# Attention values as float32 matmuls in four column groups, and the first layer norms' normalisation moved from VectorE to GpSimd

## What is computed

```python
xn = layer_norm(layernorm(x), norm_g, norm_b)          # (32, 128, 128)
xfn = layer_norm(ctx_768, tnorm_g, tnorm_b)            # (32, 77, 96)
q, k, v = xn @ Wq + bq, xfn @ Wk + bk, xfn @ Wv + bv   # 16 heads of 8
w = softmax(q @ k.T / sqrt(8))
x = x + tanh(g_xattn) * (w @ v)
xf = layernorm(x)
top_vals, top_idx = top_k(xf @ w_router, 2)            # of 8 experts
h = square(relu(xf @ w1[e]))                           # for every expert
y = sum over the two chosen of (h @ w2[e]) * softmax(top_vals)
x = x + tanh(g_ffn) * y
```

## Time and profile before

| what | before |
|---|---|
| median of 3 runs | 432.58 us (431.52 to 435.71) |
| profiled execution | 432.84 us |
| its span on the core | 431.0 us |
| mean granted TensorE clock | 0.761 |
| busy: TensorE, VectorE, ACT, GpSimd | 72%, 68%, 52%, 51% |

### The profile page before, as it was taken

One profiled execution on the slowest core, in us unless ns is written; L12 is line 12 of the kernel. 1 busy time (PEld: TensorE's weight loads), 2 busy tenths in 40 slices (PEclk: granted clock), 3 DMA queues, 4 the chain that ended last, 5 costly groups with the idle time before them and its releaser, 6 DMA issues.

```text
span 431.0 us, 9014 instructions
## 1 busy us (share of the span) xinstructions
PE 309.2 (72%) x2664; PEld 261.7 (61%) x2664; DVE 291.7 (68%) x956; ACT 224.9 (52%) x490; POOL 221.8 (51%) x261
## 2 busy tenths in 40 slices
PE   0502693779399849885997869885888599699566
PEld 0301472667388738874786748774777488587455
DVE  5524744875577787868785787877887678847432
ACT  1210353556356765676565646764576467665222
POOL 8601353664566555755573458545754565665100
PEclk9965555555559975998598958995999589769869
DMA  2346019001831075206530382229211821050140
GB/s 51 100 87 93 2 44 142 5 2 42 143 125 75 33 116 157 106 28 105 159 119 8 78 170 75 75 75 159 96 75 57 146 97 78 27 198 2 47 174 24
DMA packets 29314, 36.57 MB, mean 85 GB/s; under 512 B 5849, under 2 KB 22874, under 8 KB 29274
## 3 DMA queue, kind: packets, MB, share of 16 engines
q1 hardware_dynamic: 28474, 35.05, 33.1%
q0 software_dynamic: 512, 1.06, 0.9%
q10 hardware_dynamic: 288, 0.00, 0.0%
HBM read 23.14 MB, written 2.23 MB: 59 GB/s over the span
## 4 chain that ended last, share of the span: by engine, by line
PE 39%; DVE 23%; issue 13%; DMA 11%; SPq 5%; POOL 4%; ACT 3%; DVEq 1%; POOLq 0%; ACTq 0%
PE y L533 10%; DMA qs<-q_lo 8%; PE ab L455 6%; PE s L477 5%; SPq L313 4%; DVE u L947 3%; DVE negm L831 3%; PE c L493 3%; DVE xn L782 3%; PE h L524 2%; PE ab L437 2%; DMA gb<-gates_scratch 2%; PE h L526 2%; PE h L525 2%; DVE x L867 2%
## 5 line engine op out<-in xcount | busy, mean ns | idle before, releaser
L1079 POOL TENSOR_TENSOR p_lo<-p,p_hi 77x512 f16<-77x512 f32 x128 | 147.8, 1158 | 109.9 <-ACT p L681 109.7
L831 DVE TENSOR_REDUCE negm<-ab 128x4 f32<-128x308 f32 x128 | 58.9, 470 | 72.7 <-PE ab L455 69.8
L455 PE MATMUL ab<-ks,qs 96*128 96x312 f32 x128 | 62.8, 495 | 39.8 <-DMA qs<-q_lo 27.4
L680 ACT ACTIVATE p_hi<-s 77x512 f16<-77x512 f32 x128 | 74.8, 585 | 31.2 <-PE s L477 30.9
L533 PE MATMUL y<-w2s,hs 128*128 128x128 f32 x512 | 74.2, 293 | 6.1 <-ACT hs L688 6.0
L477 PEld LDWEIGHTS s<-qs,ks 104*77 104x77 f32 x512 | 70.1, 194 | 10.9 <-issue 4.8
L681 ACT ACTIVATE p<-s 77x512 f32<-77x512 f32 x128 | 74.8, 584 | 0.0
L533 PEld LDWEIGHTS y<-w2s,hs 128*128 128x128 f32 x512 | 67.5, 206 | 8.1 <-ACT hs L688 7.4
L477 PE MATMUL s<-qs,ks 104*77 104x128 f32 x512 | 72.0, 280 | 0.2 <-ACT p L681 0.2
L455 PEld LDWEIGHTS ab<-ks,qs 96*128 96x128 f32 x128 | 31.1, 244 | 47.0 <-issue 33.9
L688 ACT ACTIVATE hs<-u 128x512 f32<-128x512 f32 x64 | 40.2, 628 | 31.3 <-DVE u L947 29.1
(11 more groups left out here) (100 smaller groups left out, 503.7 us busy)
## 6 DMA issues: line engine op xcount, KB each, us to landing
gb<-gates_scratch SPq DMA_DIRECT2D x16, 768.0 KB, 4.2
qs<-q_hi SPq DMA_DIRECT2D x16, 256.0 KB, 5.7
gb<-gates_scratch SPq DMA_DIRECT2D x8, 512.0 KB, 3.6
ks<-k_hi SPq DMA_DIRECT2D x64, 39.0 KB
x_sb<-in_x_dram SPq DMA_DIRECT2D x8, 256.0 KB, 6.7
qs<-q_lo SPq DMA_DIRECT2D x8, 256.0 KB, 6.9
x_res<-in_x_dram SPq DMA_DIRECT2D x8, 256.0 KB, 6.8
out_dram<-y_out SPq DMA_DIRECT2D x8, 256.0 KB, 5.8
```

Of the source, the lines that this page charges most:

```text
L455: nc.tensor.matmul(p[:, 0:J * NP].rearrange("t (i n) -> t i n", n=NP), qs[0:QR, par, c, T * j:T * j + T], ks[0:QR, par, c, :, NP * j:NP * ...
L680: nc.scalar.activation(p_hi[:, c, :], src, ACT.Exp).then_inc(hi_done, 1)
L831: nc.vector.tensor_reduce(negm[:, :, c], bank_ab[bank][:, 0:J * NP].rearrange("t (i n) -> t i n", n=NP)[:, :, 0:N], AX.X, ALU.max, negate= ...
L1079: nc.gpsimd.tensor_tensor(p_lo[:, c, :], p32[:, c, :], p_hi[:, c, :], ALU.subtract).then_inc(lo_done, 1)
```

## The change

1. **Exponentials.** ACT writes only `p32`; `p_hi`, `p_lo` and GpSimd's `low_part` are gone.
2. **Values.** The roles are turned round: `vs` is stationary and `p32` moves, both plain float32. Each head has 32 stationary columns, of which either the first 16 or the last 16 are used (8 features, the ones, 7 zeros) and the others are zero. The four heads of a chunk go to partitions 0, 32, 64 and 96 of bank `c`, which are four column groups of the array. Two chunks add into the same 128 columns, one with the first 16 rows of every group, the other with the last 16. The output has features on partitions.
3. **Turning back.** ACT copies the 128x256 of bank `c` to `oT` (`evacuate_heads`), TensorE turns it in two transposes (`turn_heads`) into a bank `ab`, with four new uses in `AB_USES`, and VectorE's reciprocal and multiplication read from there. The addition of the three parts is gone.
4. **v.** ACT writes v straight into `vs` in two instructions (even and odd heads); the three splitting steps are gone. GpSimd clears `vs` and writes the ones at the start.
5. **First layer norms.** GpSimd runs `normalise` (four instructions for the context, four for x) right behind each root; VectorE's `normalise_ctx` and `normalise_x` are gone. VectorE's `take(post)` is one place later.

```diff
-        vs = sb("vs", [N, 2, G, H, VC], BF16)
+        vs = sb("vs", [N, 2, G, H, VT])
-        p_hi = sb("p_hi", [N, LR, CH * T], F16)
-        p_lo = sb("p_lo", [N, LR, CH * T], F16)
+        oT = sb("oT", [CH * VT, 2 * T])
...
@@ -483,17 +475,27 @@
                 if c == 0:
-                    pe.wait_ge(split_v, at(SPLIT, s, "lo"))
+                    bank, k = ab(s, "v")
+                    pe.wait_ge(v_done, s + 1)
+                    pe.wait_ge(ab_taken[bank], k)
+                    if not loop and n == 0:
+                        pe.wait_ge(v_ones, ONES)
                     if loop or n > 0:
-                        pe.wait_ge(post_d, at(POST, n - 1, "recip"))
-                pe.wait_ge(lo_done, m + 1)
+                        pe.wait_ge(o_taken, n)
+                pe.wait_ge(p_done, m + 1)
+                r = T * (c // 2)
                 for i in range(J):
-                    h, k = NC * i + c, T * i
-                    for part in (p_hi, p_lo):
-                        mm = nc.tensor.matmul(bank_c[:, VC * h:VC * h + VC], part[:, c, k:k + T],
-                                              vs[:, par, j, h, :], start=(c == 0 and i == 0 and part is p_hi),
-                                              stop=(part is p_lo), skip_group_check=True)
+                    mm = nc.tensor.matmul(bank_c[VT * i:VT * i + VT, r:r + T], vs[:, par, j, NC * i + c, :],
+                                          p32[:, c, T * i:T * i + T], start=(c == 0), stop=(c % 2 == 1),
+                                          skip_group_check=True)
                 mm.then_inc(pv_done, 1)
+
+            def turn_heads(s, par, j, loop=False):
+                pe.wait_ge(o_taken, G * s + j + 1)
+                p, ready = claim(s, f"o{j}", loop)
+                for r in range(2):
+                    mm = nc.tensor.transpose(p[:, T * r:T * r + T], oT[:, T * r:T * r + T], ident[:, :])
+                mm.then_inc(ready, 1)
...
@@ -556,6 +558,8 @@
                         scores(*near[2], 3, loop)
                     if near[0]:
                         scoresT(*near[0], 1, loop)
+                    if near[-1]:
+                        turn_heads(*near[-1], loop)
                     if e[0] is not None:
                         hidden(sf, pf, e[0], loop)
...
-                nc.scalar.activation(vs[:, par, :, :, 0:HD * PARTS].rearrange("n b h (d a) -> n a (b h) d", a=PARTS)[:, 0],
-                                     bank_ab[bank][0:N, :].rearrange("n (c d) -> n c d", d=HD), ACT.Copy,
-                                     scale=col(GX, N)).then_inc(hi_v, 1)
-                if loop or s > 0:
-                    act.wait_ge(split_v, at(SPLIT, s - 1, "rest"))
-                nc.scalar.activation(v32[:, :, :].rearrange("n b d -> n (b d)"), bank_ab[bank][0:N, :], ACT.Copy,
-                                     scale=col(GX, N)).then_inc(ab_taken[bank], 1)
+                for odd, done in enumerate((v_done, ab_taken[bank])):
+                    k = VC * odd
+                    nc.scalar.activation(vs[:, par].rearrange("n b (m o) k -> n o (b m) k", o=2)[:, odd, :, k:k + HD],
+                                         bank_ab[bank][0:N, :].rearrange("n (m o d) -> n o m d", o=2, d=HD)[:, odd],
+                                         ACT.Copy, scale=col(GX, N)).then_inc(done, 1)
+
+            def evacuate_heads(s, par, j):
+                act.wait_ge(pv_done, NC * (G * s + j) + NC)
+                nc.scalar.activation(oT[:, :], bank_c[:, 0:2 * T], ACT.Copy).then_inc(o_taken, 1)
...
@@ -677,7 +685,6 @@
                 if loop or m >= LR:
                     act.wait_ge(pv_done, m - LR + 1)
                 src = bank_s2[c % 2][0:N, :]
-                nc.scalar.activation(p_hi[:, c, :], src, ACT.Exp).then_inc(hi_done, 1)
                 nc.scalar.activation(p32[:, c, :], src, ACT.Exp).then_inc(p_done, 1)
...
                 dve.wait_ge(stats_d, at(STATS, s, "x_stats"))
+                if loop or s > 0:
+                    dve.wait_ge(normed, at(NORM, s - 1, "x_normed"))
...
@@ -845,26 +817,25 @@
             def attended(s, par, j, loop=False):
 
                 n = G * s + j
-                dve.wait_ge(pv_done, NC * n + NC)
-                view = bank_c[:, 0:VC * H].rearrange("t (h v) -> t h v", v=VC)
-                nc.vector.tensor_reduce(o[:, :].rearrange("t (h d) -> t h d", d=HD),
-                                        view[:, :, 0:HD * PARTS].rearrange("t h (d a) -> t h d a", a=PARTS),
-                                        AX.X, ALU.add).then_inc(post_d, 1)
+                bank, k = ab(s, f"o{j}")
+                view = bank_ab[bank][:, 0:VC * H].rearrange("t (h v) -> t h v", v=VC)
+                dve.wait_ge(ab_ready[bank], k)
                 nc.vector.reciprocal(rden[:, :].rearrange("t (h o) -> t h o", o=1),
-                                     view[:, :, HD * PARTS:VC]).then_inc(post_d, 1)
+                                     view[:, :, HD:HD + 1]).then_inc(post_d, 1)
                 yield
                 dve.wait_ge(post_d, at(POST, n, "recip"))
-                nc.vector.tensor_tensor(o[:, :].rearrange("t (h d) -> t h d", d=HD),
-                                        o[:, :].rearrange("t (h d) -> t h d", d=HD),
+                nc.vector.tensor_tensor(o[:, :].rearrange("t (h d) -> t h d", d=HD), view[:, :, 0:HD],
                                         rden[:, :].rearrange("t (h o) -> t h o", o=1).broadcast_to([T, H, HD]),
-                                        ALU.mult).then_inc(post_d, 1)
+                                        ALU.mult).then_inc(ab_taken[bank], 1)
                 yield
                 if j == 0:
                     dve.wait_ge(res_in[par], landed(s, par))
                     if loop or s >= 2:
                         dve.wait_ge(y_added, s - 1)
-                dve.wait_ge(post_d, at(POST, n, "scaled"))
-                nc.vector.tensor_tensor(x1[:, par, j, :], x_res[:, par, j, :], o[:, :], ALU.add).then_inc(post_d, 1)
+                dve.wait_ge(ab_taken[bank], k)
+                nc.vector.tensor_tensor(x1[:, par, j, :].rearrange("t (i r e) -> t i r e", i=J, r=2),
+                                        x_res[:, par, j, :].rearrange("t (i r e) -> t i r e", i=J, r=2),
+                                        o[:, :].rearrange("t (r i e) -> t i r e", i=J, r=2), ALU.add).then_inc(post_d, 1)
...
-                    if j == 1 and nxt:
-                        prepare = split_values(*nxt, loop)
-                    if j == 3 and third:
-                        prepare = chained(normalise_ctx(*third, loop), normalise_x(*third, loop))
...
-                    take(post)
                     take(top_scores)
                     if near[-2]:
                         routed(*near[-2])
                     take(top_scores)
+                    take(post)
                     take(post)
                     if near[-2]:
...
-            def low_part(s, par, j, c):
-
-                m = NC * (G * s + j) + c
-                pool.wait_ge(hi_done, m + 1)
-                pool.wait_ge(p_done, m + 1)
-                nc.gpsimd.tensor_tensor(p_lo[:, c, :], p32[:, c, :], p_hi[:, c, :],
-                                        ALU.subtract).then_inc(lo_done, 1)
+            def normalise(s, par, which):
+                src, dst, n, mv, k, name = {"ctx": (ctx_sb, cn, N, c_mv, 1, "crstd"),
+                                            "x": (x_sb, xn, T, x_mv, 3, "rstd")}[which]
+                pool.wait_ge(norm_p, at(NORM_P, s, name))
+                apart(pool)
+                for b in range(G):
+                    ins = nc.gpsimd.tensor_scalar(dst[:, b, :], src[:, par, b, :], mv[:, b, 0:1],
+                                                  nrm[0:n, k, b:b + 1], ALU.subtract, ALU.mult)
+                ins.then_inc(normed, 1)
...
+            nc.gpsimd.memset(vs[:, :, :, :, :], 0.0).then_inc(v_ones, 1)
+            pool.wait_ge(v_ones, 1)
+            for odd in range(2):
+                k = VC * odd + HD
+                nc.gpsimd.memset(vs[:, :, :, :, :].rearrange("n p b (m o) k -> n o (p b m) k", o=2)[:, odd, :, k:k + 1],
+                                 1.0).then_inc(v_ones, 1)
...
@@ -1123,20 +1097,13 @@
                         load_experts()
                     if j == 3 and third:
                         norm_rstd(third[0], "ctx")
-                    if near[0]:
-                        low_part(*near[0], 0)
-                    if j == 3 and third:
+                        normalise(*third, "ctx")
                         norm_rstd(third[0], "x")
+                        normalise(*third, "x")
                     if j == 1 and exists(i - 1, loop):
                         gate_roots(i - 1)
-                    if near[0]:
-                        low_part(*near[0], 1)
                     if near[-1]:
                         rstd(*near[-1])
-                    if near[0]:
-                        low_part(*near[0], 2)
-                    if near[0]:
```

(1 more changed line is left out.)

80 lines of the change are left out of this document (21 added, 59 removed).

## The result

The changed kernel takes 468.21 us (median of four runs, 464.73 to 470.78), the kernel before beside it on the same chip 432.05 us (431.19 to 435.71). The ratio is 1.081, with a 95% interval of 1.072 to 1.091: 36 us slower. The prediction said 436 us, range 419 to 472. The time lies inside the range, and the sign that I held likelier came; the case that I called likeliest did not. The trace of the changed kernel is of the fastest of its four runs, 464.73 us: its span is 462.9 us where the kernel before has 431.0, so the traces show 31.9 of the 36 us.

A forecast was written before the change was run, and what follows sets the result against it. Bound by transfers (some 19 us of each 45 us tile) and TensorE's work (some 26). TensorE stretches +5.1, two earlier ones +2, beginning +2 and -2, end -4.5 and +1: +3.6 on 432.84, 436 us (chance 0.35); range 419 to 472.

The forecast's parts named there:

- the sign that I held likelier: Whole kernel slower than before by over 1%: chance 0.50, against 0.30 faster and 0.20 within 1%.
- What bounds the kernel: Per 45 us tile, some 19 us set by transfers up to q_lo (transfer stretch), some 26 by TensorE's work (TensorE stretch).
- Chunks at 0.22 us, groups beside each other: Values of four heads on TensorE: column groups overlap, 0.22 us at full, 0.43 at half clock; +0.9 us per TensorE stretch.
- the drain rival: Each values chunk pays two TensorE drains of 0.15 us for changing tiling mode; 16 us more, 452; chance 3%.
- Turning, 0.24 us per batch, "I count no wait": Two TensorE transposes per batch turn heads back: 0.24 us full, 0.48 half clock, no wait for ACT's copy; 0.96 per stretch.
- The clock stays as it is: First 10 of a TensorE stretch's 25.7 us stay at half clock; about four chunks run at half, seven at full.
- Half of the 8.5 us idle comes back: TensorE stretches: half of the 8.5 us idle over five stretches comes back as shorter waits, -4.2 us.
- GpSimd's normalisations, 0.45 us each: 64 layer-norm normalisations moved to GpSimd: 0.45 us each, 6.2 us with the roots, in a slot of 11 us.
- Beginning and end: Beginning: about +2 us for clearing and normalisations, -2 for lost p_lo latency; end: -4.5, +1 for chunks and turns.
- Rival 1: Slower: passes in program order, only neighbouring column groups overlap; chunk 0.54 us full, 1.05 half clock; 467 or 460; chance 0.20.
- Rival 2: Slower: column groups do not overlap; chunk 0.86 us full, 1.68 half clock; 497 or some 480 us; chance 0.15.
- Rival 3: Faster: all stretch idle, end's 4.7 us and beginning's 4 us go, chunks stay 0.20 us; -12.4, 420 us; chance 0.27.

The follow-up runs named there:

- e10: Changed kernel without the heads' copy and turning transposes (attention values wrong), normalisations back on VectorE; 443.8 us, 1.018 of the kernel before.
- e3: Changed kernel with the heads turned later, behind the third scoresT, and VectorE's part behind the gating; 464.6 us, 1.072 of the kernel before.
- e12: Changed kernel with normalisations back on VectorE and the heads turned behind the slot's first hidden layer; 458.4 us, 1.056 of the kernel before.
- e4: Changed kernel with all four heads of a chunk in one column group (three quarters of attention values left out); 548.6 us, 1.264 of the kernel before.

## Why the prediction was right and wrong, step by step

- **What bounds the kernel** (two stretches per tile): right. The transfer stretch kept its 17.7 us, q_lo's wait took the gates' place, and every steady us lost is in the TensorE stretch.
- **Chunks at 0.22 us, groups beside each other**: right for a chunk in the middle of a visit. At half clock two chunks take 1.02 us (271.38 to 272.40), twice the forecast's 0.43 and 0.16 for the exit. The step lacked the price of entering and leaving, 0.22 us per visit. I had weighed it as the drain rival, read the earlier trace rows as showing none, and gave it 3%. A cost of that kind exists, at about three quarters of the 0.30 us that I put on it, but paid per visit, not per chunk; whether it is a drain stays open. By itself it decided little: e10, which has all visits, has before's period, since the waits that went pay for them.
- **Turning, 0.24 us per batch, "I count no wait"**: this step failed, and it is the largest part of the miss against 436 us. I looked for ACT's copy of bank c, and rightly found it hidden (383 ns, 0.2 us of waits in all). I didn't ask for the other half of the claim, the bank itself. The use before the last is the router's, which VectorE takes behind 0.48 us of maxima. The runs show 0.88 us per turn instead of 0.24. With VectorE's normalisations, leaving the turning out is worth 21 of 29 us. The wait is shown by the trace; that it is most of the 21 us is not, as moving it away brought back only 4 to 5 us (e3, e12), and part of the rest is the clock.
- **The clock stays as it is** ("the idle time before it stays"): the premise held, 4.49 us of idle time for 3.38 and 0.88, and the conclusion did not in two of the four tiles. The half-clock part after the first scores lasted 15.2 and 14.1 us, not 10, and 8.0 and 9.7 in the other two; in e10 it lasted about 9. Six chunks of the tile shown ran at half clock, not four.
- **Half of the 8.5 us idle comes back**: in e10, TensorE is busy 27.13 of 27.30 us in this stretch, so nearly all came back, and the chunks took it. In the changed kernel the turning's wait is larger than what came back.
- **GpSimd's normalisations, 0.45 us each**: mis-sized. They take 0.69 and 0.82 us, between the bounds. In the steady tiles they fit into the slot, as said; in the first two tiles they stand on the path, 5.9 us by the second query projection. I had put all of the beginning at +2 - 2.
- **Beginning and end**: the first query projection is 4.9 us later, of which 3.7 is the clearing, as computed. The second is 9.5 us later, which I hadn't computed: 6.1 us stand at the first tile's scores (42.70 for 36.60), the rest is GpSimd's chain. The end's -3.5 did not come: from the eighth projection (+25.9) to the end 6 us more are lost.
- **Rival 1** gave 467, and the time is 468. That is a coincidence: its mechanism, 0.54 us per chunk, is absent. Nor is it more than luck that 468 lies in a range whose upper part was drawn for rivals 1 and 2. Rival 2 is excluded by e4. Rival 3's waits were indeed worth more than I took, but the chunks and visits took what they gave.
- **What stays open**: e10 still loses 8 us. 3.8 are the clearing at the start, and one tile (from 192.60 to 243.74) is 51.1 us long for before's 46.9, with TensorE's clock at 0.72 over its stretch for 0.79. In it TensorE waits 3.10 us for the maxima (2.32 before), which VectorE begins late for no reason that the trace shows:

```profile
233.06 0.86 DVE L817 TENSOR_REDUCE negm<-ab 128x4 f32<-128x308 f32 x2 [3.10 <-issue]
```

  Behind it half the clock is granted from 232.2 to 242.4 us, where the kernel before has 3.4 us of it (228.7 to 232.1). Turned heads in a bank of their own were not tried either, so no run shows whether the turning can be had without its wait.
